# Experts and second attention ordered by batch in a four-block transformer kernel

## Chip, cores and metric

The kernel runs on one core of a Trainium2 chip. The metric is the device time of one execution in microseconds (us), the median of several runs.

## The reference

The input has B = 2 sequences of S = 1024 tokens with D = 128 features. Four blocks follow each other, each of the form x = x + layernorm(block(layernorm(x))):

```
x = x + ln(attn0(ln(x)))     # 16 heads of 64, causal softmax
x = x + ln(moe(ln(x)))       # 8 experts, top 2, capacity 1.25, gelu, F = 256
x = x + ln(attn1(ln(x)))     # 16 heads of 8, rotary q and k, causal; a score of exactly 0 is masked
x = x + ln(ffn(ln(x)))       # ternary weights, squared relu, low-rank term
```

The second attention:

```
q, k = rope(x @ Wq), rope(x @ Wk);  v = x @ Wv          # 16 heads of 8
scores = q @ k.T / sqrt(8) * tril;  scores = where(scores == 0, -inf, scores)
out = softmax(scores) @ v @ wo.T
```

The router ranks a token among all tokens of both sequences (an expert keeps the first CAP of them), so routing needs all of x. Nothing after routing mixes the two batches.

## The kernel before

The kernel is written per engine: TensorE (`pe`), VectorE (`dve`), ScalarE (`act`), GpSimd (`pool`) and the DMA queue of SyncE (`sp`) each have an instruction list in a fixed order, tied by semaphores. Tokens are handled in 16 tiles of 128; a PSUM bank holds 4 tiles (512 tokens, 2 KB per partition), so the two batches are 4 banks (`NB`), and `bank[0..7]` are the eight PSUM banks.

Attention 0 (to 562 us) and its output projection and norms are not touched. After them the router (VectorE) picks experts.

**Experts.** For each of 8 experts `up(e)` makes 8 bank products (2 feature chunks x 4 token banks) in banks 0 to 3 in turn, ScalarE applies gelu into `hT` (double buffered), `down(e)` makes four banks 4 to 7, and VectorE adds each, weighted, into `acc` (`weighted_sums`). TensorE's order is `up(e+1)`, `down(e)`. All 2048 tokens go through one expert before the next. Experts 1 to 6 run in a hardware loop of two per turn on each engine; in it VectorE copies the weights' column and the bias column of the expert (`wcol`, `b1e`). SyncE loads w1 and w2 of the expert after next.

**Between experts and attention 1.** Norm 2 (`norm_stage(2, ...)`): moments and scaling of the experts' sum, GpSimd's power for 1/sqrt and its addition to X, then moments and scaling of X to `xn`. TensorE transposes a bank of it, ScalarE copies it to `xnT`, TensorE makes five projections per bank (q, q with swapped halves, k, k swapped, v), ScalarE copies each from PSUM (`rot`, `V1`). For each of four arrays i (q and k of batch 0, q and k of batch 1, 1024 columns each) VectorE multiplies by the cosine (L996), GpSimd the swapped one by the sine (L533), VectorE adds (L1002). The sum is split in three bf16 parts: ScalarE casts a part (`part`, L667), VectorE subtracts it (`left`, L991), and again; the last part is VectorE's own. The parts are stored to DRAM (`split`), and `stacks(b, g)` loads the part products of a group of 4 heads: 18 loads of 64 KB that fill `QS[:, b]` and `KS[:, b]` (72 partitions, all 9 pairs of parts). So scores of 8 features become one bf16 matmul over 72 rows.

**Attention 1** is 256 items (group of heads, batch, query tile, head). Per step i: TensorE scores(i); VectorE `mask` (L818) makes `Zb`, a large negative number where a score is zero, and `maximum` (L833) adds it and takes the row maximum; ScalarE the exponential (L605) into `probs`; TensorE transposes them (L1133), ScalarE copies them to `PT` (L585), and after every fourth item TensorE multiplies by V. One group of heads takes 64 items: batch 0 with its query tiles rising, then batch 1 with them falling. Thus both batches must be ready before the first group is done. `self.rounds` lists everything that goes through the three PSUM banks `pT`, and `at_step` the step of each.

Order before: group 0 batch 0, group 0 batch 1, group 1 batch 0, and so on. `NMASK = 4` buffers hold `Zb` and `Sm`.

The block after (norm 3, feed-forward, norm 4) is not touched.

Of the kernel before, what the change touches and what calls it, by code (L numbers as in the profile page):

```python
# [7 lines left out]

# [14 lines left out]
P = 128  # L23
B, S, D = 2, 1024, 128
T = B * S
# [21 lines left out]
PROJ1 = (0, 1, 2, 3, 6, 7)  # L47
QUEUED = 4
NMASK = 4
# [32 lines left out]

class Attention:
# [3 lines left out]
    def __init__(self, heads, turns, copies, project):  # L87
# [3 lines left out]
        self.order = [(c, b, qt) for c in range(turns) for b, qt in order]  # L91
        self.items = [(c, b, qt, h) for c, b, qt in self.order for h in range(heads)]
# [12 lines left out]
        for step in range(self.n + 8):  # L105
# [5 lines left out]
            if project:  # L111
                c, at = divmod(step, self.per)
                for c2, b2, start in ((c, 1, 1), (c + 1, 0, self.per // B + 1)):
                    u, odd = divmod(at - start, 2)
                    if 0 <= u < 6 and not odd and c2 < turns:
                        self.project(step, c2, b2, u)
            self.done_by.append(dict(self.copied))
# [4 lines left out]
    def add(self, step, what, args, engines):  # L122
        for e in engines:
            self.copied[e] += 1
        self.at_step[step].append(len(self.rounds))
        self.rounds.append((what, args, {e: self.copied[e] for e in engines}))

# [37 lines left out]
def build(nc, x, w0, wo0, router_w, router_b, w1, b1, w2, b2, wl1, wo1, fast_bT, w_fc, w_proj, uT, v, gate,  # L165
          consts, rotary, out):
    with ExitStack() as ctx:
# [28 lines left out]
        hT = at(0, "hT", [P, 2, FC0, T])  # L196
# [11 lines left out]
        Sm = at(48, "Sm", [P, NMASK, S])  # L208
        cs = at(56, "cs", [P, 2, S])
        QS = at(64, "QS", [P, B, HPG, S], BF16)  # L210
        KS = at(80, "KS", [P, B, HPG, S], BF16)
        rot = at(96, "rot", [P, 8, S])
        PT1 = at(96, "PT1", [P, 2, HPG, S])
        parts = at(136, "parts", [P, 2, PARTS, S], BF16)
# [32 lines left out]
        wcol = sb("wcol", [P, 2, NT])  # L247
# [9 lines left out]
        b1e = sb("b1e", [P, 2, FC0])  # L257
# [52 lines left out]
        rope, rope_sin, part_a, part_v, part_stored = sem("rope"), sem("rope_sin"), sem("part_a"), sem("part_v"), [sem("part_stored0"), sem("part_stored1")]  # L310
        ld_stack = [sem("ld_stack0"), sem("ld_stack1")]

        b1_ready = sem("b1_ready")
# [7 lines left out]
        wcol_ready = sem("wcol_ready")  # L321
# [8 lines left out]
        L = [Attention(HPC, CH0, ["act", "dve"], True), Attention(HPG, G1, ["act"], False)]  # L330
        block = ctx.enter_context(nc.Block())
# [3 lines left out]
        def _(sp):  # L335
# [63 lines left out]
            sp.dma_start(cs[:, :, :], rotary).then_inc(ld_rot, 16)  # L399
            sp.dma_start(wo1s[:, :, :], wo1).then_inc(ld_wo1, 16)  # L400

            with sp.Fori(0, E // 2 - 1) as t:
                for e in range(2):
                    sp.wait_ge(up_done, (t * 2 + e) * UNITS + UNITS)
                    sp.dma_start(w1s[:, e, :], w1[bass.ds(t * 2 + 2 + e, 1), :, :].rearrange("o p f -> p (o f)")).then_inc(ld_w1[e], 16)
                    sp.wait_ge(down_done, (t * 2 + e) * NB + NB)
                    sp.dma_start(w2s[:, e, :, :], w2[bass.ds(t * 2 + 2 + e, 1), :, :].rearrange("o (c p) d -> p (o c) d", p=P)).then_inc(ld_w2[e], 16)
            def stacks(b, g):
# [5 lines left out]
                for i in range(PARTS):  # L414

                    for j in range(PARTS):
                        row = (i * PARTS + j) * DH1
                        sp.dma_start(QS[row:row + DH1, b, :, :], heads(0, slice(i, i + 1)).rearrange("k d h s -> (k d) h s"))\
                            .then_inc(ld_stack[b], 16)
                        sp.dma_start(KS[row:row + DH1, b, :, :], heads(1, slice(j, j + 1)).rearrange("k d h s -> (k d) h s"))\  # L420
                            .then_inc(ld_stack[b], 16)

            for i in range(2):
                sp.wait_ge(part_a, 2 * i + 2)
                sp.wait_ge(part_v, 2 * i + 2)
                sp.dma_start(split[i, :, :, 0:S].rearrange("k p s -> p k s"), parts[:, i, :, :]).then_inc(part_stored[i], 16)
            for b in range(B):
                for i in range(2):  # L430
                    sp.wait_ge(part_stored[i], 16 * (b + 1))
                stacks(b, 0)
            for g in range(G1 - 1):
                for b in range(B):
                    sp.wait_ge(A[1]["s"], g * L[1].per + (b + 1) * L[1].per // B)
                    stacks(b, g + 1)
# [8 lines left out]
        def _(pool):  # L445
# [83 lines left out]
            powers(2)  # L529
            pool.wait_ge(ld_rot, 16)  # L530
            for i in range(4):
                pool.wait_ge(proj1_copied, 5 * (i // 2 * 2 + 1) + i % 2 * 2 + 2)
                pool.tensor_tensor(rot[:, 2 * i + 1, :], rot[:, 2 * i + 1, :], cs[:, 1, :], ALU.mult).then_inc(rope_sin, 1)  # L533
# [5 lines left out]
        def _(act):  # L539
# [23 lines left out]

            def factors_out(a, g):
# [4 lines left out]
            def attention(k):  # L569
                a, plan = A[k], L[k]  # L570
                PT = PT0 if k == 0 else PT1
                def rounds_out(i):
                    for r in plan.at_step[i]:
# [4 lines left out]
                        if what == "P":  # L578
                            projected(a, args, pT[r % TBANKS][:, :])
                            continue  # L580
# [28 lines left out]
                for i in range(plan.n + QUEUED + 1):  # L609
# [5 lines left out]
                    else:  # L615
                        rounds_out(i)
                        exponential(i)

# [20 lines left out]
            def gelus(e, buf):  # L639

                act.wait_ge(b1_ready, e + 1)
                for u in range(UNITS):
                    f, j = u % FC0, u // FC0
                    act.wait_ge(up_done, e * UNITS + u + 1)
                    nc.scalar.activation(hT[:, buf, f, j * BANK:(j + 1) * BANK], bank[u % 4], ACT.Gelu,  # L645
                                         bias=b1e[:, buf, f:f + 1]).then_inc(h_ready, 1)

            gelus(0, 0)
# [687 lines left out]
```

## Time and profile before

| | before |
|---|---|
| median of 3 runs | 1271.85 us (1269.1 to 1274.05) |
| profiled execution, its own time | 1276.66 us |
| its span in the trace | 1274.7 us |
| busy over the span: TensorE / VectorE / ScalarE / GpSimd | 1114.3 / 869.6 / 817.2 / 348.9 us |
| mean granted TensorE clock | 0.955 of full speed |
| experts (first `up` after routing to last sum) | 625.9 to 732.5 us |
| gap from the experts to the first scores of attention 1 | to 801.7 us |
| attention 1, to its output projection | to 1209.6 us |

A busy share says how long an engine had an instruction under way. Its average over the kernel mixes stages with different limits; the rows below are therefore taken by stretch. The granted clock has two levels: 1.00 is 2.4 GHz and 0.50 is 1.2 GHz.

### The profile page before, as it was taken

To read this page: it belongs to the slowest core of one execution; us is meant where nothing else is said; L and a number is where in the kernel's file an instruction comes from. 1 tells how busy PE (TensorE), PEld (TensorE's weight loads), DVE (VectorE), ACT (ScalarE), POOL (GpSimd) and SP (SyncE) were. 2 spreads that over 40 slices of the span, in tenths; PEclk is the share of its full clock that TensorE was granted. 3 is DMA by queue.
4 is the path that set the end of the run, shared out by engine and by line. 5 is a ranking of instruction groups with operands and counts; after the bars stand their busy time and mean duration, and the time that the engine had idled before them with its cause. 6 is when DMAs were issued, how large, how long until landed. Compare 5 with 4: busy or idle time off the path is not lost.

```text
span 1274.7 us, 28360 instructions
## 1 busy us (share of the span) xinstructions
PE 1114.3 (87%) x10202; PEld 850.3 (67%) x10202; DVE 869.6 (68%) x2512; ACT 817.2 (64%) x1915; POOL 348.9 (27%) x345
## 2 busy tenths in 40 slices
PE   2799999999999999998999951688888888888886
PEld 1587888787878787888676730456556556556674
DVE  3565656565656665645433476799899999999863
ACT  2566666666666666631434223789889989989832
POOL 1597464646464545313000051000000000000033
PEclk9899999999999999998899976799899999899998
DMA  3222232323232222211000004311302202100001
GB/s 107 70 60 62 69 73 59 83 57 84 57 76 66 69 72 68 67 35 42 5 17 25 5 1 118 56 24 17 39 12 29 38 4 37 27 14 2 2 1 33
DMA packets 29671, 56.74 MB, mean 45 GB/s; under 512 B 4538, under 2 KB 14674, under 8 KB 29410
## 3 DMA queue, kind: packets, MB, share of 16 engines
q1 hardware_dynamic: 28738, 53.43, 18.8%
q8 instruction: 80, 1.31, 0.4%
q10 hardware_dynamic: 800, 1.57, 0.4%
q14 instruction: 53, 0.43, 0.1%
HBM read 25.49 MB, written 4.33 MB: 23 GB/s over the span
## 4 chain that ended last, share of the span: by engine, by line
PE 55%; DVE 19%; issue 11%; ACT 6%; POOL 5%; DMA 3%; SPq 1%; ACTq 0%; POOLq 0%; DVEq 0%
PE pT L1133 12%; PE pO L1063 11%; PE pS L1100 10%; DVE Zb L818 9%; PE pS L1195 4%; PE pT L1025 4%; PE pT L1207 3%; DVE Sm L833 3%; ACT probs L605 3%; PE pS L1156 2%; PE pT L1029 2%; PE pS L1293 1%; PE pS L1273 1%; ACT PT L585 1%; DMA KS<-split 1%
## 5 line engine op out<-in xcount | busy, mean ns | idle before, releaser
L1133 PE MATMUL pT<-cst,probs 128*128 128x128 f32 x2304 | 368.8, 286 | 55.2 <-ACT probs L605 53.2
L1133 PEld LDWEIGHTS pT<-cst,probs 128*128 128x128 f32 x2304 | 255.5, 142 | 151.9 <-ACT probs L605 104.0
L605 ACT ACTIVATE probs<-probs,nmax 128x128 f32<-128x128 f32 (+7 forms) x256 | 198.8, 776 | 131.7 <-DVE nmax L828 130.7
L585 ACT COPY PT<-pT 128x512 f32<-128x512 f32 (+3 forms) x576 | 263.7, 481 | 16.1 <-PE pT L1133 14.7
L828 DVE CUSTOM_DVE_ANT_0 probs<-pS,causal_wide 128x128 f32<-128x128 f32 (+7 forms) x256 | 192.1, 750 | 92.8 <-PE pS L1100 85.2
L1063 PE MATMUL pO<-PT,V 128*64 128x128 f32 (+1 forms) x4608 | 230.6, 277 | 1.9 <-DVE attnT L787 1.1
L605 ACT ACTIVATE probs<-Sm,nmax 128x128 f32<-128x128 f32 (+7 forms) x256 | 199.2, 778 | 29.3 <-DVE nmax L833 22.3
L818 DVE TENSOR_SCALAR Zb<-pS 128x128 bf16<-128x128 f32 (+7 forms) x256 | 192.8, 753 | 24.4 <-PE pS L1106 24.1
L461 POOL TENSOR_TENSOR rstd<-rstd,power 128x4 f32<-128x4 f32 x32 | 32.8, 1025 | 628.0 <-DVE rstd L725 627.4
L1063 PEld LDWEIGHTS pO<-PT,V 128*64 128x64 f32 (+1 forms) x4608 | 179.9, 113 | 33.8 <-issue 19.6
L833 DVE CUSTOM_DVE_ANT_0 Sm<-pS,Zb 128x128 f32<-128x128 f32 (+7 forms) x256 | 193.3, 755 | 4.5
L862 DVE COPY PT<-pT 128x256 f32<-128x256 f32 (+3 forms) x192 | 99.9, 520 | 115.9 <-PE pT L1133 114.5
L1100 PE MATMUL pS<-Kh,Qs 128*128 128x512 f32 (+2 forms) x384 | 159.0, 423 | 7.2 <-DMA Kl<-Kl 7.2
L1100 PE MATMUL pS<-KS,QS 72*128 72x512 bf16 (+3 forms) x384 | 109.0, 338 | 36.0 <-DMA KS<-split 31.9
L1100 PE MATMUL pS<-Kl,Qs 128*128 128x512 f32 (+2 forms) x384 | 128.8, 344 | 0.0
L1100 PEld LDWEIGHTS pS<-Kh,Qs 128*128 128x128 f32 x384 | 73.3, 191 | 27.8 <-issue 21.7
L1100 PEld LDWEIGHTS pS<-Kl,Qs 128*128 128x128 f32 x384 | 73.5, 191 | 20.3 <-issue 14.6
L645 ACT ACTIVATE hT<-pS,b1e 128x512 f32<-128x512 f32 x64 | 43.9, 687 | 57.5 <-PE pS L1195 57.3
L504 POOL TENSOR_TENSOR Kl<-raw,Kh 64x512 fp32r<-64x512 f32 x60 | 76.5, 1276 | 4.8
L504 POOL TENSOR_TENSOR Ql<-raw,Qs 64x512 fp32r<-64x512 f32 x60 | 76.5, 1275 | 4.8
L524 POOL TENSOR_TENSOR attnT<-attnT,wq_t 128x1024 f32<-128x1024 f32 x16 | 37.9, 2370 | 117.6 <-DMA wq_t<-factors 117.0
L976 DVE SCALAR_TENSOR_TENSOR acc<-pT,wcol,acc 128x128 f32<-128x128 f32 x96 | 27.0, 344 | 61.7 <-PE pT L1207 61.7
(185 smaller groups left out, 1376.2 us busy)
## 6 DMA issues: line engine op xcount, KB each, us to landing
Qs<-Ql SPq DMA_DIRECT2D x32, 256.0 KB, 3.7
Kh<-Kh SPq DMA_DIRECT2D x32, 256.0 KB, 3.4
Kl<-Kl SPq DMA_DIRECT2D x32, 256.0 KB, 4.6
wq_t<-factors SPq DMA_DIRECT2D x32, 256.0 KB, 3.9
QS<-split SPq DMA_DIRECT2D x72, 64.0 KB
KS<-split SPq DMA_DIRECT2D x72, 64.0 KB
w0s<-in_w SPq DMA_DIRECT2D x8, 192.0 KB, 4.1
split<-parts SPq DMA_DIRECT2D x2, 768.0 KB, 3.5
```

The costliest lines, as they stand in the source:

```text
L504: i = pool.tensor_tensor(low[h], source[rows[h], :], high[h].bitcast(F32), ALU.subtract)
L585: nc.scalar.copy(PT[:, g % 2, h, k0 * P:(k0 + nk) * P], pT[r % TBANKS][:, 0:nk * P])\
L605: nc.scalar.activation(probs[:, i % NPROB, 0:n], src[:, 0:n], ACT.Exp, bias=nmax[:, i % 4:i % 4 + 1], scale=-1.0, accum_out=total).then_in ...
L818: nc.vector.tensor_scalar(Zb[:, i % NMASK, 0:n], pS[i % 2][:, 0:n], 0.0, MASKED, ALU.is_equal, ALU.mult).then_inc(a["z"], 1)
L828: nc.vector.tensor_tensor_reduce(probs[:, i % NPROB, 0:n], pS[i % 2][:, shift(k, qt):shift(k, qt) + n], causal_wide[:, S - n:S], -1.0, 3e3 ...
L833: nc.vector.tensor_tensor_reduce(Sm[:, i % NMASK, 0:n], pS[i % 2][:, 0:n], Zb[:, i % NMASK, 0:n], -(DH1 ** -0.5), 3e38, ALU.add, ALU.min, ...
L862: nc.vector.tensor_copy(PT[:, gg % 2, hh, k0 * P:(k0 + nk) * P], pT[r % TBANKS][:, 0:nk * P])\
L1025: return nc.tensor.matmul(p, w0s[:, what, :], xnT[:, b * S + j * BANK:b * S + (j + 1) * BANK], start=True, stop=True)
L1063: m = nc.tensor.matmul(pO[rows, 0:P], v, PT[:, g % 2, h, kt * P:(kt + 1) * P], start=(kt == 0), stop=(kt == qt), skip_group_check=True)
L1100: m = nc.tensor.matmul(pS[i % 2][:, (off + c0) * P:(off + c1) * P], lhs, keys[:, b, h, c0 * P:c1 * P], start=(n == 0), stop=(n == len(rhs) ...
L1133: m = nc.tensor.transpose(pT[r % TBANKS][:, kt * P:(kt + 1) * P], probs[:, item % NPROB, (k0 + kt) * P:(k0 + kt + 1) * P], ident)
L1195: nc.tensor.matmul(bank[u % 4], w1s[:, buf, f * P:(f + 1) * P], xnT[:, j * BANK:(j + 1) * BANK], start=True, stop=True).then_inc(up_done, 1)
```

## The change

The experts run over batch 0 (m = 0 to 7) and then over batch 1 (m = 8 to 15), each step with half the tokens: 4 banks of `up`, 2 of `down`. While batch 1 is in the experts, batch 0 goes through norm 2, transposes, projections, rotation, split and stacked loads. Attention 1 takes all four groups of batch 0 and then all of batch 1; norm, projections, rotation and split of batch 1 are written into the steps of its first 64 items, by tables.

- The hardware loops and the copies `wcol` and `b1e` are gone; weights are loaded 16 times instead of 8 in all (14 after the first two).
- From m = 8 on `up` uses banks 0 and 1 alone, `down` banks 4 and 5 (before m = 8: 0 to 3, and 4 to 7 in pairs). Banks 2 and 3, then 6 and 7 serve transposes and projections.
- ScalarE casts the parts of batch 0 between the gelus of expert steps 13 and 14 (first part) and 14 and 15 (second).
- `QS` and `KS` have two buffers as before, now for this half and the next one of the order. `rot`, `parts` and others have new places in SBUF; `NMASK` is 3 to make room.
- SyncE waits for both stores of batch 0 and then issues stacks(0) and stacks(1) one behind the other. The stores of batch 1 follow stacks(2). Before, ScalarE's queue stored batch 1.

Core of the diff:

```diff
-NMASK = 4
+NMASK = 3
+NORM_STEPS = {1: ("ym", 2), 2: ("ym", 3), 4: ("yn", 2), 5: ("yn", 3), 7: ("xm", 2), 8: ("xm", 3), 10: ("xn", 2), 11: ("xn", 3)}
+ROTATE_STEPS = {38: ("cos", 2), 39: ("cos", 3), 41: ("add", 2), 42: ("add", 3), 44: ("left", 2, 0), 47: ("left", 2, 1),
+                53: ("left", 3, 0), 57: ("left", 3, 1)}
+PART_STEPS = {43: (2, 0), 46: (2, 1), 51: (3, 0), 55: (3, 1)}
+SECOND_BATCH = collections.defaultdict(list)
+for _j in (2, 3):
+    SECOND_BATCH[11 + _j].append(("N", _j))
+    for _what in range(5):
+        SECOND_BATCH[16 + 2 * ((_j - 2) * 5 + _what)].append(("Q", (_j, _what)))
...
+        if heads > 2:
+            self.order = [(c, b, qt) for b in range(B) for c in range(turns) for qt in (tiles if c % 2 == 0 else reversed(tiles))]
...
+            store(0)
+            store(1)
+            sp.wait_ge(part_stored, 32)
+            stacks(0)
+            stacks(1)
+            for half in range(2, G1 * B):
+                sp.wait_ge(A[1]["s"], (half - 1) * (L[1].per // B))
+                if half == G1:
+                    sp.wait_ge(part_stored, 64)
+                stacks(half)
+                if half == 2:
+                    store(2)
+                    store(3)
...
+            for m in range(1, B * E):
+                gelus(m)
+                if m == E + 3:
+                    for j in range(2):
+                        act.wait_ge(tr_done[2], j + 1)
+                        nc.scalar.copy(xnT[:, j * BANK:(j + 1) * BANK], bank[2 + j]).then_inc(xnT_ready[2], 1)
+                if m in (E + 3, E + 4):
+                    j = m - E - 3
+                    for what in range(5):
+                        u = j * 5 + what
+                        act.wait_ge(proj1, u + 1)
+                        projected1(j, what, bank[PROJ1[u % len(PROJ1)]]).then_inc(proj1_copied, 1)
+                if m in (E + 5, E + 6):
+                    part(0, m - E - 5)
+                    part(1, m - E - 5)
...
+            for m in range(E):
+                sums(m, (0, 1))
+            for what in ("ym", "yn", "xm", "xn"):
+                second_norm(what, 0)
+                second_norm(what, 1)
+                if what != "xn":
+                    sums(E + "ym yn xm xn".split().index(what) // 2, ("ym yn xm xn".split().index(what) % 2,))
+            sums(E + 1, (1,))
+            sums(E + 2, (0, 1))
+            sums(E + 3, (0, 1))
+            rotate("cos", 0)
+            rotate("cos", 1)
+            sums(E + 4, (0, 1))
+            rotate("add", 0)
+            rotate("add", 1)
+            left(0, 0)
+            left(1, 0)
+            sums(E + 5, (0, 1))
+            left(0, 1)
+            left(1, 1)
+            sums(E + 6, (0, 1))
+            sums(E + 7, (0, 1))
...
+            for m in range(B * E):
+                if m + 1 < B * E:
+                    up(m + 1)
+                if m == E + 2:
+                    pe.wait_ge(h_ready, E * per_batch)
+                    for j in range(2):
+                        transpose1(j, bank[2 + j]).then_inc(tr_done[2], 1)
+                down(m)
+                if m in (E + 2, E + 3):
+                    j = m - E - 2
+                    pe.wait_ge(xnT_ready[2], 2)
+                    pe.wait_ge(added, NT + E * ST)
+                    for which in range(5):
...
+                        project1(j, which, bank[PROJ1[u % len(PROJ1)]]).then_inc(proj1, 1)
```

`second_norm`, `rotate` and `left` are the pieces of the norm, the rotation and the split as before, one bank or one array at a time. In the inner loop of TensorE, "N" transposes a bank of the normalized batch 1 and "Q" makes one projection, both through `pT`; ScalarE copies them out in its own list.

## Rows read from the trace of the kernel before

**Rows 1.** Busy time by stretch (us, instructions): TensorE, its weight loads, VectorE, ScalarE, GpSimd; clock, DMA.

```profile
732.00:803.00 71.00, 23.26 (x86) 13.25 (x86) 45.56 (x127) 21.27 (x33) 23.48 (x16) 0.68 0.23 62
803.00:1209.00 406.00, 347.69 (x4156) 241.87 (x4154) 387.73 (x955) 370.64 (x961) 0.00 (x0) 0.96 0.16 22
```

**Rows 2.** Chain that ended last, experts: start us, us, engine, output, line, instructions.

```profile
625.90 7.06 PE pS L1195 x16
...
654.12 6.87 PE pS L1195 x16
660.99 5.36 PE pT L1207 x48
...
668.13 6.87 PE pS L1195 x16
```

**Rows 3.** Timeline, a gelu and the last weighted sum (start us, us, idle before).

```profile
626.99 0.69 ACT L645 ACTIVATE hT<-pS,b1e 128x512 f32<-128x512 f32 x1 [4.12 <-PE pS L1195]
...
731.37 1.13 DVE L976 SCALAR_TENSOR_TENSOR acc<-pO,wcol,acc 128x128 f32<-128x128 f32 x4 [0.66 <-PE pO L1207]
```

**Rows 4.** Timeline of VectorE, norm 2.

```profile
732.41 0.86 DVE L718 BATCH_NORM_STATS2 stats<-acc 128x6 f32<-128x128 f32 x4
...
733.80 0.86 DVE L718 BATCH_NORM_STATS2 stats<-acc 128x6 f32<-128x128 f32 x4
...
735.19 1.11 DVE L731 TENSOR_SCALAR yn<-acc,mv,rstd 128x128 f32<-128x128 f32 x4
736.21 0.86 DVE L718 BATCH_NORM_STATS2 stats<-acc 128x6 f32<-128x128 f32 x4
```

**Rows 5.** Timelines of VectorE, ScalarE and GpSimd, rotation and split.

```profile
758.08 0.59 ACT L683 COPY rot<-pS 128x512 f32<-128x512 f32 x1 [0.27 <-PE pS L1260]
758.80 4.85 POOL L533 TENSOR_TENSOR rot<-rot,cs 128x1024 f32<-128x1024 f32 x2 [7.91 <-ACT rot L683]
...
764.66 1.21 DVE L996 TENSOR_TENSOR rot<-rot,cs 128x1024 f32<-128x1024 f32 x1
764.77 1.05 ACT L667 CAST parts<-rot 128x1024 bf16<-128x1024 f32 x1 [2.21 <-DVE rot L1002]
765.85 1.23 DVE L991 TENSOR_TENSOR rot<-rot,parts 128x1024 f32<-128x1024 f32 x1
```

**Rows 6.** Timelines, from the last split pass of batch 0 to the first scores.

```profile
776.21 1.23 DVE L991 TENSOR_TENSOR parts<-rot,parts 128x1024 bf16<-128x1024 f32 x1
...
781.05 0.29 SPq L418 DMA_DIRECT2D QS<-split  x1
...
801.73 0.26 PE L1100 MATMUL pS<-KS,QS 72*128 72x128 bf16 x1 [31.88 <-DMA KS<-split]
```

**Rows 7.** Busy time by stretch around one set of stacked loads in the attention.

```profile
850.00:852.00 2.00, 2.00 (x47) 1.72 (x38) 2.00 (x3) 1.95 (x5) 0.00 (x0) 1.00 0.49 87
...
866.00:868.00 2.00, 1.45 (x12) 0.94 (x10) 2.00 (x6) 1.98 (x5) 0.00 (x0) 1.00 0.36 50
```

**Rows 8.** Busy time by stretch: items 0 to 15, 16 to 31, 32 to 51.

```profile
802.00:820.50 18.50, 14.97 (x120) 8.85 (x119) 15.46 (x57) 15.28 (x48) 0.00 (x0) 0.74 0.54 65
820.50:853.40 32.90, 28.36 (x331) 19.29 (x330) 32.63 (x63) 29.24 (x67) 0.00 (x0) 1.00 0.06 11
853.40:891.90 38.50, 33.48 (x458) 25.05 (x456) 38.16 (x78) 36.73 (x84) 0.00 (x0) 1.00 0.21 25
```

**Rows 9.** Waits in attention 1: total us, times, longest.

```profile
ACT probs L605 <- DVE nmax L833: 22.3, 77, 0.5
```

**Rows 10.** TensorE and ScalarE around routing, and the clock after the experts.

```profile
609.43 9.14 PE L1195 MATMUL pS<-xnT,w1s 128*128 128x512 f32 x16
...
615.18 0.69 ACT L645 ACTIVATE hT<-pS,b1e 128x512 f32<-128x512 f32 x1 [0.17 <-PE pS L1195]
...
618.89 0.23 PE L1217 MATMUL pT<-selb,upperb 128*128 128x128 bf16 x1 [0.32 <-DVE beforeb L936]
...
736.00:737.00 1.00, 0.00 (x0) 0.00 (x0) 1.00 (x6) 0.00 (x0) 1.00 (x2) 0.69 0.00 0
```

More of the change, by code:

```diff
@@ L116, in __init__ @@
                         self.project(step, c2, b2, u)
+            if not project:
+                for r, args in SECOND_BATCH[step]:
+                    self.add(step, r, args, ["act"])
             self.done_by.append(dict(self.copied))
@@ L1005, in _, with sums @@
-            dve.wait_ge(proj1_copied, 20)
+            def sums(m, banks):
+                for j in banks:
+                    dve.wait_ge(down_done, m * 2 + j + 1)
+                    dve.wait_ge(added, NT + ((m - 1) * ST + (j + 1) * TPB if m % E else 0))
+                    for t in range(TPB):
+                        n = m // E * ST + j * TPB + t
+                        nc.vector.scalar_tensor_tensor(acc[:, n, :], bank[down_bank(m, j)][:, t * P:(t + 1) * P],
+                                                       wgt[:, n, m % E:m % E + 1], acc[:, n, :], ALU.mult, ALU.add).then_inc(added, 1)
@@ L1214, in _, with up @@
-            up(0, 0, first=True)
+            def up(m):
+                pe.wait_ge(ld_w1[m % 2], 16 * (m // 2 + 1))
+                for u in range(per_batch):
+                    f, j = u % FC0, m // E * 2 + u // FC0
+                    if m >= 1:
+                        pe.wait_ge(h_ready, m * per_batch + u - 1 if m > E or u >= 2 and m == E else m * per_batch + u - 3)
+                    nc.tensor.matmul(bank[u % 4 if m < E else u % 2], w1s[:, m % 2, f * P:(f + 1) * P],
+                                     xnT[:, j * BANK:(j + 1) * BANK], start=True, stop=True).then_inc(up_done, 1)
@@ new lines, in down @@
+            def down(m):
+                pe.wait_ge(ld_w2[m % 2], 16 * (m // 2 + 1))
+                for j in range(2):
+                    last = m - 2 if m <= E else m - 1
+                    pe.wait_ge(h_ready, m * per_batch + FC0 * (j + 1))
+                    pe.wait_ge(added, NT + (last * ST + (j + 1) * TPB if last >= 0 else 0))
+                    for t in range(TPB):
+                        for f in range(FC0):
+                            n = j * TPB + t
+                            i = nc.tensor.matmul(bank[down_bank(m, j)][:, t * P:(t + 1) * P],
+                                                 hT[:, m % 2, f, n * P:(n + 1) * P], w2s[:, m % 2, f, :],
+                                                 start=(f == 0), stop=(f == FC0 - 1))
+                    i.then_inc(down_done, 1)
```

341 lines of the change are left out of this document (159 added, 182 removed).

## Prediction

> **What bounds the kernel now.** I read the profile from the stages inward. The busy table by stretch [rows 1] has the two stretches that the change touches. Between 732 and 803 us TensorE works 23.3 of 71 us: nothing there keeps any engine full. From 803 to 1209 us, the second attention, VectorE is busy 387.7 of 406 us, ScalarE 370.6, TensorE 347.7: VectorE sets the pace, and what is added to it there costs nearly its own length.
>
> Before 732 us the chain that ended last is TensorE alone [rows 2]: an `up` of 8 banks takes 6.87 us, a `down` of 4 banks 668.13 - 660.99 = 7.14, one expert 14.01 us. Halved for one batch: `up` 3.44, `down` 3.57, expert 7.01; one bank of `down` 1.79. VectorE adds a bank in 1.13 us, and the last one starts at 731.37; a gelu takes 0.69 us and starts right behind its bank [rows 3].
>
> The gap itself is a string of latencies. The norm of a bank [rows 4] is moments 733.80 - 732.41 = 1.39 us and the scaling 736.21 - 735.19 = 1.03, each done twice (for the output and for the next input): 4.84 us a bank. Then come projections, and the rotation with its split in three parts [rows 5]: on VectorE four passes of 1024 elements, 765.85 - 764.66 = 1.19 us each, ScalarE's casts 1.05, GpSimd's product with the sine 4.85 / 2 = 2.43, a projection's copy 0.59. Last come the stores and stacked loads [rows 6]: the second store of batch 0 is released by the pass that ends at 776.21 + 1.23 = 777.44, the loads start at 781.05 (3.6 us later), and TensorE begins at 801.73, after 31.88 idle us that end with a stacked load.
>
> **The change, step by step.** Experts run batch by batch. Up to the boundary nothing but the grain changes: eight half experts, 8 x 7.01 = 56.1 us from 625.90, so at 682.0. The shorter `up(0)` lies under the router on VectorE, thus it gives nothing; the other 15 halves are 105.2 of `up` and `down` in a longer loop than before by half an `up`, 3.4 us. Weights are loaded 14 times instead of 6, 128 KB each, on an otherwise idle queue, with at least 7 us from issue to use; free.
>
> Then I lay out batch 1, counting from t = 0 at 682.0, with these durations. TensorE: `up(9)` and `down(8)` to 7.0, `up(10)`, `down(9)` to 14.0, `up(11)` to 17.5. VectorE meanwhile: last sum of expert 7 to 1.2, two moments to 3.9, sum (5.3 to 6.4), two scalings to 8.5, sum to 9.5, moments to 12.3, sum to 13.4, scalings to 15.5, sum to 16.6. The transposes at 17.5 find their inputs ready, and `down(10)` its bank. So the norm of batch 0, 9.7 us of VectorE, costs TensorE no wait. Transposes 1.2, `down(10)` to 22.3, five projections at 0.86 (one bank of `up`, 6.87 / 8) to 26.6; `up(12)`, `down(11)` to 33.6, five projections to 37.9; `up(13)`, `down(12)` to 44.9.
>
> Here comes the one wait I find. VectorE's sum ends at 46.1 and only then its two additions of the rotation, at 47.3 and 48.5. ScalarE stands in order before the gelus of expert 14 with two casts that wait for these: they end at 49.5. With two banks left to `up`, TensorE's third bank waits until 50.3 where it would have started at 46.6: 3.6 us. `up(14)` ends at 52.0, `down(13)` at 55.6, its sum at 56.7, then the last two passes of the split at 57.9 and 59.1. Two banks instead of four also cost some 0.25 us per expert, since a bank's gelu ends 0.14 + 0.69 us after the bank and the other bank takes 0.86; with hand-overs I add 2.1 us for the six experts up to here. The second store is released at 682.0 + 61.2 = 743.2, the stacked loads start 3.6 us later, 746.8.
>
> How long do 18 stacked loads take? With two stores beside them, 801.73 - 781.05 = 20.7 us; in the attention, alone, transfers go from the slice at 850 into the one at 866 [rows 7], about 17.5. I take 19.2: attention starts at 766.0 in place of 801.7, **35.7 us sooner**. The experts end on TensorE at 682.0 + 68 = 750, so it is the split and its loads that are late, by 16 us, not the experts.
>
> Batch 1's own work now goes into VectorE's attention: norms of two banks, 9.7 us, and 8 passes, 8 x 1.19 = 9.6 us: 19.3. Of it some 2 us fall on the first small tiles, where VectorE is idle 3.0 of 18.5 us in the first row of [rows 8]: 17.3. ScalarE gets 2 + 10 copies and 4 casts, 12 x 0.59 + 4 x 1.05 = 11.3 us. In steps 16 to 31 (second row of [rows 8]) it is busy 29.2 of 32.9 us, and nine copies, nearer 0.5 each where they overlap, put it at 33.7. TensorE is busy 28.4 there, and nine of the ten projections at 0.86 put it at 36.1, in front of both; as its busy time counts the modelled tail of each group, I take a bit less: +3.0. In the falling half behind it (its third row) VectorE carries the 9.6, ScalarE has 36.7 + 4.7 and TensorE 33.5 + 0.9 of 38.5 + 9.6: no cost. Two casts stand one step ahead of the pass that needs them, and there VectorE waits about 0.6 us each: +1.2. Three masks for four: in the waits of this stretch ScalarE waits 77 times for VectorE's maximum [rows 9], so it isn't three items behind; nothing. The loads of later halves have 50 us each. Sum in the attention: 17.3 + 3.0 + 1.2 = **+21.5**.
>
> Bounds: the loads 17.5 to 20.7; hand-overs and the 3.6 us wait between 0 and 8; the inserted work from 15.6 (19.3 less the 3.7 us that VectorE is idle in the three rows, and nothing else) to twice the 17.3.
>
> Sum: -35.7 + 21.5 = -14.2. The profiled execution took 1276.66 us (span 1274.7 and 2.0 around it), 4.8 over the median of 1271.85. So 1262.5 for a like execution, and 1257.7 as median, **1258**.
>
> **The rivals.**
> 1. The inserted work is hidden better: VectorE's idle 3.7 us take their part, ScalarE and TensorE keep up, the one-step waits vanish, and the loads take 17.5. For it: VectorE does idle while TensorE makes scores. Against: most of that idle time is in the smallest tiles. I take 8 us for the three: 1250.
> 2. TensorE's clock falls. `up(0)` is half as long: the gelu of its fourth bank started at 615.18, and the matmul that ranks tokens came at 618.89: some 3.9 idle us where the old `up(0)` filled them. The granted clock fell from 2.4 to 1.2 GHz some 5 us after the matmuls that ended at 731.3 (0.69 in the slice 736 to 737) [rows 10]. If it falls in this gap, the b2 products and the next `up` run slower. The old `up(0)` began in the low state and took 9.14 against 6.87 us at the full one; I take 3 us. 1261. A gap of 3.6 us before the third bank could do the same once more.
>    The Trainium skill (TensorE: Matmul & The Clock Gate, What's actually happening) calls the low rate the default, which only activity lifts; by that rule the clock falls in this gap, and the median is this rival's 1261. Whether a gap so short suffices, no row here shows.
> 3. Three engines are nearly full in the attention (388, 371, 348 of 406 us), and each inserted piece breaks their rhythm: a chunk of 1.4 us on VectorE makes ScalarE late, then TensorE's transposes, then the next scores. If that doubles the cost of 17 us, 1258 + 17 = 1275, no change.
> 4. The other side. The stacked loads of the second half now follow those of the first without a pause, 36 where 18 went. While 18 are under way the DMA engines are about half busy (0.49 in the slice at 850), so two sets could share them. If the two sets run interleaved, attention starts after both: 41.4 us for 19.2, and 1258 + 22 = 1280, slower. From 14.2 us above my 19.2 on, the gain is gone. Against it: one queue, issued in order, and before the change two stores pushed in between cost at most 3 us.
>
> **How the numbers follow.** My forecast 0.60, rival 1: 0.10, rival 2: 0.12, rival 3: 0.10, rival 4: 0.08. The range reaches to rival 1 and a bit beyond (1248) and most of the way to rival 3, whose milder half is inside: 1248 to 1273. Outside are rival 4, the other half of 3 and a lower tail. The line of 0.5% (6.4 us, about what a measurement of this kernel can tell from no change) lies at 1265.5. Forecast, 1 and 2 are below it, less 0.05 for their upper tails: faster 0.77. Most of rival 3 and the tails: same 0.13. Rival 4 and a bad end of 3: slower 0.10.
>
> **What would show it.** The boundary between batches at 682, TensorE full with one wait of 3 to 4 us in `up(14)`, released by a gelu behind casts; experts ending at 750; the first stacked load issued near 747 and the first scores near 766, TensorE idle 16 us in between. The attention from there to the output projection 429 us instead of 408, all the excess in its first two halves (about 50 each before), the other six unchanged. Wrong would be: scores only after some 785 (rival 4), more than 435 us of attention (rival 3), the clock at half after 620 (rival 2).

## The result and the profile after

The changed kernel takes 1258.2 us (median of 4 runs, 1254.7 to 1264.2) against 1273.0 for the kernel before in the same runs: the ratio is 0.989, with a 95% interval of 0.984 to 0.994. The forecast was 1258, with a range of 1248 to 1273. The profiled execution of the changed kernel is its shortest (1254.74 us, span 1252.9) and that of before one of the longer ones, so the two traces stand 21.8 us apart where the medians stand 14.7 apart. The comparison by stage must therefore say which stretches the change touched at all.

Busy time by stretch, after (us, instructions: TensorE, weight loads, VectorE, ScalarE, GpSimd; granted clock, DMA share, GB/s). The stretches are experts of batch 0, experts of batch 1, the wait for the stacked loads, the first two halves of the attention, and its other six:

```profile
626.00:684.65 58.65, 58.65 (x327) 41.94 (x326) 18.05 (x62) 21.98 (x32) 0.00 (x0) 0.97 0.11 32
684.65:753.30 68.65, 65.22 (x353) 44.22 (x351) 38.99 (x124) 31.10 (x45) 12.43 (x8) 0.98 0.16 51
753.30:769.30 16.00, 0.06 (x2) 0.07 (x2) 1.29 (x5) 0.00 (x0) 0.00 (x0) 0.58 0.55 72
769.30:890.35 121.05, 101.42 (x1073) 68.77 (x1074) 116.30 (x296) 100.81 (x251) 11.29 (x8) 0.87 0.17 33
890.35:1191.60 301.25, 255.49 (x3130) 178.53 (x3128) 291.61 (x724) 276.68 (x726) 0.00 (x0) 0.99 0.15 21
```

The 71 us of [rows 1] in which no engine was full have become 16. VectorE is busier in the second row than in the first (39.0 for 18.1 us), with the norm, rotation and split of batch 0, and TensorE is still full but for 3.4 us. In the attention VectorE is the busiest engine in both rows, 116.3 of 121.1 us in the first.

The timeline of TensorE after, at the end of the experts (start us, us, idle time before and its releaser):

```profile
735.30 3.65 PE L1299 MATMUL pS<-xnT,w1s 128*128 128x512 f32 x4 [3.43 <-ACT hT L729]
...
742.39 3.79 PE L1299 MATMUL pS<-xnT,w1s 128*128 128x512 f32 x8
746.01 7.31 PE L1312 MATMUL pT<-w2s,hT 128*128 128x128 f32 x64
769.26 0.27 PE L1198 MATMUL pS<-KS,QS 72*128 72x128 bf16 x1 [15.94 <-DMA KS<-split]
```

and those of VectorE, ScalarE and SyncE beside it:

```profile
731.23 2.35 DVE L866 TENSOR_TENSOR rot<-rot 128x1024 f32<-128x1024 f32 x2
732.48 2.18 ACT L639 CAST parts<-rot 128x1024 bf16<-128x1024 f32 x2 [5.18 <-DVE rot L866]
734.57 1.26 ACT L729 ACTIVATE hT<-pS,b1s 128x512 f32<-128x512 f32 x2
...
743.64 2.35 DVE L871 TENSOR_TENSOR parts<-rot,parts 128x1024 bf16<-128x1024 f32 x2
746.92 1.28 ACT L688 ACT_TABLE_LOAD   x1
750.50 0.30 SPq L464 DMA_DIRECT2D QS<-split  x1
```

These answer to [rows 5, 6]. The third bank of `up(14)` waits 3.43 us for a gelu; that gelu (734.57) stands behind two casts, and these behind the two additions of the rotation. The last split pass ends at 743.64 + 2.35 = 745.99, the loads start 4.5 us later and take 769.26 - 750.50 = 18.8 us, and TensorE waits 15.94 us for them. It starts 32.5 us sooner than before. One row holds something that was not forecast: ScalarE loads the table of the exponential at 746.92, far ahead of the first scores; before, this load stood between the first scores and the first exponential. The row before:

```profile
802.87 1.28 ACT L605 ACT_TABLE_LOAD   x1 [14.77 <-DVE nmax L833]
```

The attention has eight halves of 32 items. Taken from the first mask of each half to that of the next, they last 59.9, 60.8, 50.3, 50.1, 49.1, 50.1, 49.1 and 52.6 us (to the output projection) after; before, 51.2, 50.1, 51.8, 50.1, 49.1, 50.1, 52.1 and 53.0. So the inserted work costs 8.7 + 10.7 = 19.4 us between these two traces, and 4.9 us of the difference lie in halves that do the same as before. The two touched halves, the first before and after, then the second before and after:

```profile
802.00:853.40 51.40, 43.34 (x448) 28.14 (x447) 48.09 (x117) 44.52 (x114) 0.00 (x0) 0.91 0.23 30
769.60:829.55 59.95, 51.26 (x474) 32.58 (x472) 58.10 (x167) 47.38 (x123) 8.92 (x7) 0.83 0.15 22
853.40:903.50 50.10, 43.13 (x588) 32.06 (x585) 48.56 (x123) 48.08 (x123) 0.00 (x0) 1.00 0.16 20
829.55:890.35 60.80, 49.86 (x601) 35.91 (x599) 58.20 (x130) 53.43 (x129) 2.37 (x1) 0.92 0.20 43
```

VectorE's busy time grows by 10.0 and 9.6 us. The 10.7 of the second half is the figure of one execution: in the ten other profiled executions that hold all of batch 1's work on VectorE this half took 60.1 to 62.7 us (the first always 59.9), with VectorE busy 58.1 to 58.3 us in each and the clock at 1.2 GHz for a different share of the time. Against 50.1 before, the second half thus costs 10.0 to 12.5 us.

### The profile page after: what moved, and what is told of

Its sections match the earlier page's. It is cut to its first block, busy times and chain, and to the rows that moved or that the text cites. A ratio compares the mean times of both kernels' runs of the same rounds, so it can differ in the third digit from the quotient of the medians.

```text
span 1252.9 us, 28180 instructions
## 1 busy us (share of the span) xinstructions
PE 1112.5 (89%) x10202; PEld 844.8 (67%) x10202; DVE 862.9 (69%) x2486; ACT 814.4 (65%) x1915; POOL 349.4 (28%) x345
## 4 chain that ended last, share of the span: by engine, by line
PE 56%; DVE 18%; issue 11%; ACT 7%; POOL 5%; DMA 3%; SPq 1%; ACTq 0%; POOLq 0%; DVEq 0%
PE pT L1237 12%; PE pO L1160 12%; PE pS L1198 10%; DVE Zb L914 9%; PE pS L1299 4%; PE pT L1108 4%; PE pT L1312 3%; ACT probs L688 3%; DVE Sm L929 3%; PE pS L1260 2%; PE pT L1112 2%; ACT PT L668 1%; PE pS L1379 1%; PE pS L1359 1%; DMA KS<-split 1%
## 5 line engine op out<-in xcount | busy, mean ns | idle before, releaser
L688 ACT ACTIVATE probs<-Sm,nmax 128x128 f32<-128x128 f32 (+7 forms) x256 | 199.4, 779 | 61.2 <-DVE nmax L929 55.4
L914 DVE TENSOR_SCALAR Zb<-pS 128x128 bf16<-128x128 f32 (+7 forms) x256 | 192.7, 753 | 21.5 <-PE pS L1204 21.2
L1198 PEld LDWEIGHTS pS<-Kl,Qs 128*128 128x128 f32 x384 | 73.5, 191 | 20.3 <-issue 14.6
L729 ACT ACTIVATE hT<-pS,b1s 128x512 f32<-128x512 f32 x64 | 43.7, 687 | 57.2 <-PE pS L1299 57.2
L1064 DVE SCALAR_TENSOR_TENSOR acc<-pT,router,acc 128x128 f32<-128x128 f32 x112 | 31.5, 344 | 66.1 <-PE pT L1312 66.1
```

What stands on the lines that cost most here:

```text
L688: nc.scalar.activation(probs[:, i % NPROB, 0:n], src[:, 0:n], ACT.Exp, bias=nmax[:, i % 4:i % 4 + 1], scale=-1.0, accum_out=total).then_in ...
L914: nc.vector.tensor_scalar(Zb[:, i % NMASK, 0:n], pS[i % 2][:, 0:n], 0.0, MASKED, ALU.is_equal, ALU.mult).then_inc(a["z"], 1)
L1198: m = nc.tensor.matmul(pS[i % 2][:, (off + c0) * P:(off + c1) * P], lhs, keys[:, b if k == 0 else half % 2, h, c0 * P:c1 * P], start=(n == 0),
```

## Experiments

### Undoing the clock's fall

The granted clock after, in slices of 2 us from the end of `up(0)`:

```profile
614.00:616.00 2.00, 0.21 (x1) 0.00 (x0) 1.73 (x11) 0.76 (x2) 0.00 (x0) 1.00 0.26 66
616.00:618.00 2.00, 0.06 (x1) 0.07 (x2) 1.69 (x11) 0.00 (x0) 0.00 (x0) 1.00 0.00 0
618.00:620.00 2.00, 0.95 (x7) 0.51 (x8) 1.11 (x5) 0.00 (x0) 0.00 (x0) 0.86 0.00 0
620.00:622.00 2.00, 2.00 (x11) 1.23 (x10) 0.00 (x0) 1.23 (x3) 0.00 (x0) 0.50 0.03 8
```

TensorE is idle from 614.2 to 617.94, and its clock falls from 2.4 to 1.2 GHz in the slice at 618. That is rival 2. `e1_fill` fills the gap:

```diff
             up(0)
+            pe.wait_ge(ld_w1[1], 16)
+            for u in range(4):
+                nc.tensor.matmul(bank[7], w1s[:, 1, 0:P], xnT[:, 0:BANK], start=True, stop=True)
             pe.wait_ge(r_, 8 + NT)
```

> The changed kernel with four extra products of 512 columns on TensorE right behind up(0), so that it isn't idle while VectorE routes (their result is not used). Clock theory (rival 2 of the prediction): the granted clock stays at full from 614 us on, up(1) takes 3.4 us instead of 5.1, and the first up of batch 1 starts 3 to 4 us sooner against routing's end (684.65 - 617.94 = 66.7 us between the ranking product and the end of the eighth down in the changed kernel; 63 to 64 expected). Rival theory, that the longer stretch has another cause (weight loads, waits for sums): unchanged at 66.7. Total: 3 us less than the changed kernel, some 1255.

Measured: 1258.1 us, not to be told from the changed kernel. The first projection comes 87.4 us after the ranking product (704.94 - 617.50), in the changed kernel 89.0 (706.95 - 617.94). So filling gives 1.6 us there, half of what was expected. The changed kernel's clock falls twice, in the slices at 618 and 626 (0.86 and 0.56, with 1.00 at 624 between them). Filling removes the first fall and not the second, which comes after the transposes and the products over 8 rows, with TensorE busy all the time by its records (in `e1_fill` the slice at 626 is at 0.50).

What each fall costs can be read from the same products at either clock, first in the changed kernel, then in `e1_fill`:

```profile
619.27 2.61 PE L1325 MATMUL pT<-cst,router 128*8 128x128 f32 x12 [1.05 <-DVE router L1048]
621.68 1.06 PE L1325 MATMUL pO<-cst,router 128*8 128x128 f32 x4
626.68 5.17 PE L1299 MATMUL pS<-xnT,w1s 128*128 128x512 f32 x8
...
618.84 1.48 PE L1328 MATMUL pT<-cst,router 128*8 128x128 f32 x12 [1.05 <-DVE router L1048]
620.15 0.60 PE L1328 MATMUL pO<-cst,router 128*8 128x128 f32 x4
624.44 5.40 PE L1299 MATMUL pS<-xnT,w1s 128*128 128x512 f32 x8
633.25 3.60 PE L1299 MATMUL pS<-xnT,w1s 128*128 128x512 f32 x8
```

The first fall costs 3.67 - 2.08 = 1.6 us, the second 5.17 - 3.60 = 1.6 (1.8 in `e1_fill`): together 3.2 us in the changed kernel. In the four other profiled executions with the gap where the clock was back by 624, the distance was 89.0 to 89.3 us. In two (`e3_late` and `e6_pe8`, the same up to here) the clock stayed low to about 634, and it was 93.2 and 92.3 us. The slice at 630 in `e6_pe8`:

```profile
630.00:632.00 2.00, 2.00 (x3) 0.70 (x3) 0.39 (x1) 0.36 (x1) 0.00 (x0) 0.50 0.00 0
```

Against `e1_fill` the gap thus costs 1.6 to 5.7 us, differing from execution to execution; the second fall, which filling leaves, comes on top.

`e8_up1` fills it with work that is needed anyway:

```diff
             up(0)
+            up(1)
             pe.wait_ge(r_, 8 + NT)
...
-                if m + 1 < B * E:
+                if 0 < m and m + 1 < B * E:
                     up(m + 1)
...
             gelus(0)
+            gelus(1)
```

> The changed kernel with up(1) ahead of the routing products instead of behind them, so that eight banks of up lie under VectorE's routing as before the change. Clock theory: TensorE's idle time of 3.7 us there is filled with work that was needed anyway, so 3.4 us less behind routing, and the clock stays up as in the kernel before (1.6 us less than the changed kernel and up to 5 in its slower executions). First projection 84 us behind the ranking product (89.0 in the changed kernel, 87.4 with filling products); median 5 us less, 1253. Rival (ScalarE's gelus delay its copies for routing): 2 us or less.

Measured: 1255.5 us, ratio to before 0.985 (0.981 to 0.989). The first projection comes at 84.9 us (702.79 - 617.87), 4.1 less than in the changed kernel, near the 84 expected. Of these, 3.6 us are `up(1)` itself, no longer behind routing; the second fall of the clock came here too (0.56 in the slice at 626). As the profiled execution had 21.1 us of loads instead of 18.8, its first scores come only 1.9 us sooner.

### Which chain sets the start of the attention

`e2_early` moves VectorE's pieces, nothing else:

```diff
             rotate("cos", 1)
-            sums(E + 4, (0, 1))
             rotate("add", 0)
             rotate("add", 1)
+            sums(E + 4, (0, 1))
             left(0, 0)
             left(1, 0)
-            sums(E + 5, (0, 1))
             left(0, 1)
             left(1, 1)
+            sums(E + 5, (0, 1))
```

> The changed kernel with VectorE's two rotation additions ahead of the sums of step 12 and the last split passes ahead of the sums of step 13. Theory (the chain norm, projections, rotation, split, loads of batch 0 sets the start of the second attention, the experts don't): the 3.4 us wait of TensorE in up(14) is gone, the last split pass ends 8 us sooner (738 for 746), the first scores come 8 us sooner (761 for 769), the median falls by 8 us. Rival (the experts' end or the loads behind set the start): the wait goes but the first scores move by less than 4 us.

Measured: 1255.7 us, ratio to before 0.989 (0.985 to 0.993). TensorE's wait in `up(14)` is gone. VectorE's timeline in it:

```profile
735.74 2.36 DVE L871 TENSOR_TENSOR parts<-rot,parts 128x1024 bf16<-128x1024 f32 x2 [1.88 <-ACT parts L639]
738.02 2.15 DVE L1064 SCALAR_TENSOR_TENSOR acc<-pT,router,acc 128x128 f32<-128x128 f32 x8
```

The last split pass ends at 738.1, 7.9 us sooner, as expected; but the first scores come at 764.9, only 4.4 sooner. The rest went in two places behind it. From the split to the first load 5.7 us pass for 4.5, because SyncE issues the stores in order behind the last w2 load, which waits for `down(13)`; and the loads took 21.1 us for 18.8. So the chain of the split does set the start, but not all of what it gains arrives. My expectation of 8 us was too high by these two.

### What sets the time of 18 stacked loads

`e3_late` holds the second set back until the first scores:

```diff
             stacks(0)
+            sp.wait_ge(A[1]["s"], 1)
             stacks(1)
```

> The changed kernel, but the 18 loads of the second half are issued only after the first scores. Rival 4 of the prediction (the two sets share the DMA engines): the first 18 loads land clearly sooner than the 18.8 us of the changed kernel, and the first scores come sooner. Theory (one queue, in order): 18 to 19 us as before, no change of the median.

Measured: 1258.7 us; the loads take 775.54 - 754.81 = 20.7 us. Rival 4 is out: without the second set behind them they are not shorter (18.8 in the changed kernel, 21.0 to 21.1 in the five other executions of this order with one queue and the second set behind).

`e4_twoq` issues the nine loads of keys from ScalarE's queue, which is idle there:

```diff
+                        if half == 0:
+                            continue
                         sp.dma_start(KS[row:row + DH1, half % 2, :, :], heads(1, slice(j, j + 1)).rearrange("k d h s -> (k d) h s"))\
                             .then_inc(ld_stack[half % 2], 16)
...
+            act.wait_ge(part_stored, 32)
+            for i in range(PARTS):
+                for j in range(PARTS):
+                    row = (i * PARTS + j) * DH1
+                    act.dma_start(KS[row:row + DH1, 0, :, :],
...
+                        .then_inc(ld_stack[0], 16)
             attention(1)
```

> The changed kernel, with the nine loads of keys of the first half issued by ScalarE's queue instead of SyncE's. If the 18.8 us are set by one queue working through 18 loads one behind the other, they fall to some 10 to 12 us and the median by 7 us. If they are set by the DMA engines that hold these rows (half of them were busy), they stay at 18 us and nothing changes. I give the first 0.5.

Measured: 1258.8 us. In its timeline both queues issue from 751.21, and the scores come at 769.4:

```profile
751.21 3.42 SPq L464 DMA_DIRECT2D QS<-split  x10
...
769.40 0.26 PE L1207 MATMUL pS<-KS,QS 72*128 72x128 bf16 x1 [15.37 <-DMA KS<-split]
```

18.2 us, and 18.5 in `e7_best` below, which loads in the same way. That is next to nothing against the 18.8 of the changed kernel, but that execution is an exception: the eight others with one queue, two of them in the old order, took 20.3 to 21.1. So a second queue is worth between nothing and some 3 us, not the 7 of the expectation, and what it is worth stays open; the medians (1258.8 for 1258.2) don't tell.

Then `e9_cols` asks whether it is bytes or rows:

```diff
-            stacks(0)
+            stacks(0, slice(0, BANK), ld_first)
+            stacks(0, slice(BANK, S))
             stacks(1)
...
-                    if k == 1 and i % (plan.per // B) == 0:
+                    if k == 1 and i == 0:
+                        pe.wait_ge(ld_first, 16 * 2 * PARTS * PARTS)
+                    if k == 1 and (i == TPB * HPG or i > 0 and i % (plan.per // B) == 0):
```

> The changed kernel, with the first half's stacked loads in two sets: columns 0 to 511 of all 18 first (scores of item 0 wait for these alone), then columns 512 to 1023 (item 16 waits for them). Rows of 1 KB instead of 2 KB. If the loads are set by bytes, the first scores come after 9 to 10 us instead of 18.8 (or 21), and the median falls by 9 us. If they are set by the number of rows moved, both sets take 18 us each, the first scores come as before, and the second set is late or just in time for item 16 (some 26 us later): no change or slower. I give bytes 0.4.

Measured: 1250.5 us, ratio to before 0.983 (0.980 to 0.986). From the first load (749.55) to the first scores (760.63) 11.1 us pass, for half the bytes in the same number of rows. So the bytes count and not the rows alone, though not in proportion: half the bytes take 0.59 of 18.8 us, and a quarter (`e11_sets` below) 7.6 us, of which the issues alone take 6.2. While whole sets are under way the engines are half busy and move some 72 GB/s (third row of the first table). And the rising half needs only the first columns for its first 16 items. The first two halves keep their length (59.9 and 61.6 us), so item 16 does not wait.

### What the inserted work costs

`e5_dve8` shrinks VectorE's pieces for batch 1 and keeps their waits: in moments and scalings one tile with 8 columns, in the rotation and the first split pass 8 columns. So batch 1 is left mostly uncomputed.

```diff
-                nc.vector.tensor_tensor(to, rotated(i, 0), part_of(i)[:, j, :], ALU.subtract).then_inc(part_v, 1)
+                c = slice(0, S if i < 2 or j == 1 else 8)
+                nc.vector.tensor_tensor(to[:, c], rotated(i, 0)[:, c], part_of(i)[:, j, c], ALU.subtract).then_inc(part_v, 1)
```

> The changed kernel, leaving out nearly all of VectorE's work for batch 1 inside the attention: moments and scalings of one tile with 8 columns instead of four with 128, cosine, addition and first split pass on 8 columns instead of 1024, with all waits and the last split passes kept (so batch 1 is computed from other numbers). The inserted VectorE work falls from 19.3 to about 5 us. Theory (VectorE sets the pace, inserted work costs its own length): the first two halves of the attention, 120.7 us in the changed kernel, fall by 13 to 15 us, the first half by about 7, the second by 7. Rival 3 (rhythm broken by waits and by the other engines): they fall by less than 8 us.

Measured: 1247.6 us. The first two halves take 53.7 + 55.7 = 109.4 us, 11.3 less than after. VectorE's busy time in them:

```profile
772.50:826.30 53.80, 50.20 (x475) 33.06 (x473) 51.28 (x131) 47.49 (x123) 8.94 (x7) 0.86 0.19 25
826.30:882.00 55.70, 45.65 (x601) 33.73 (x600) 52.07 (x130) 52.91 (x129) 2.37 (x1) 1.00 0.23 48
```

It fell by 116.3 - 103.4 = 12.9 us, and the time by 11.3. That is short of the 13 to 15 I expected, but over the 8 of rival 3. The first half is the cleaner test, as its length was 59.9 us in all eleven executions with the full work, at whatever clock: 6.2 us less for 6.8 us of busy time, so VectorE's inserted work costs nearly its length. In the second half (5.1 us less) the clock is at 1.00, where the changed kernel had 0.92, so some of that can be the clock's. There ScalarE also comes up to VectorE once VectorE's part is gone (52.9 to 52.1).

`e6_pe8` shrinks TensorE's pieces for batch 1 instead (one transpose of four, projections of 8 columns), so batch 1 is transposed and projected only in part:

```diff
-                for t in range(TPB):
+                for t in range(TPB if j < 2 else 1):
...
+                if j >= 2:
+                    return nc.tensor.matmul(p[:, 0:8], wl1s[:, which, :], xnT[:, j * BANK:j * BANK + 8], start=True, stop=True)
```

> The changed kernel, leaving out most of TensorE's work for batch 1 inside the attention: one transpose instead of four per bank and projections of 8 columns instead of 512 (ScalarE's copies stay full). Theory of the prediction (in steps 16 to 31 TensorE and ScalarE come in front of VectorE, +3.0 us): the first half, 59.9 us, falls by 2 to 3 us. Rival (VectorE stays in front, the projections are hidden): by less than 0.7 us.

Measured: 1264.1 us, 5.9 more than the changed kernel, with less work. The two profiled executions are 11.5 us apart, and of these 3.3 lie behind routing, where the clock stayed low, 2.3 in the loads and 1.9 in the second half; whether the other executions were alike, nothing shows. The first half takes 59.85 us, as with the full projections. So the projections are hidden, and the rival holds: VectorE stays in front. TensorE's busy time there fell only from 51.3 to 49.4 us, though nine projections at 0.86 us were all but taken out.

`b1_nmask3` is the kernel before with `NMASK = 3`.

> The kernel before with three mask buffers instead of four. Theory: no wait of VectorE for a buffer, so the attention takes 407.8 us and the median is that of before within noise. Rival: VectorE waits for the exponential, at least 3 us more.

Measured: 1272.4 us, ratio 1.000 (0.998 to 1.002). The third buffer less costs nothing; its attention takes 404.7 us (407.8 before; 2.7 of the difference lie in one rising half, for the clock's sake, last section), its first two halves 51.2 and 50.1 as before.

### Together

`e7_best` joins `e1_fill`, `e2_early` and `e4_twoq`.

> Three edits together on the changed kernel: products behind up(0) to keep the clock, rotation and split ordered earlier, keys of the first half loaded by ScalarE's queue. If all three theories hold: 3 + 8 + 7 = 18 us less, but then the end of the experts (about 745) sets the start of the attention, so 15 us less: 1243. If the loads don't gain by a second queue: 11 us less, 1247.

Measured: 1250.0 us, ratio 0.983 (0.979 to 0.987): 3 us over the forecast for the case that the second queue gives nothing. It is 8.3 below the median of the changed kernel, where the medians of its parts alone had given 0.1, 2.5 and -0.6; with four to six runs each, 5.6 to 10.6 us apart, such medians can't be added up. In the profiled execution the first scores come 10.9 us sooner, 2.1 of them before routing. `e10_all` joins `e8_up1`, `e2_early` and `e9_cols`.

> The changed kernel with up(1) ahead of routing, rotation and split ordered earlier, and the first half's loads in two column sets. Sum of the single effects as far as they hold: 5 + 5 + 9 = 19 us less, cut by the end of the experts, which then comes near the first scores: 1243. If the column sets give nothing: 10 us less, 1248.

Measured: 1239.3 us, ratio 0.974 (0.971 to 0.976). First scores at 748.7, 20.5 us sooner than after (1.3 of them before routing), with TensorE idle for 6.0 us in front of them. `e11_sets` adds two steps:

```diff
+                if m == B * E - 1:
+                    store(0)
+                    store(1)
                 sp.wait_ge(down_done, (m - 1) * (S // BANK))
...
-            stacks(0, slice(0, BANK), ld_first)
+            stacks(0, slice(0, 2 * P), ld_first[0])
+            stacks(0, slice(2 * P, BANK), ld_first[1])
```

> The version with all three edits (up(1) ahead of routing, rotation and split earlier, loads by column sets), with two more steps: the first set is split again (columns 0 to 255 for items 0 to 7, 256 to 511 for items 8 to 15), and the two stores of batch 0 are issued ahead of the last w2 load in SyncE's order, as in that version 5.7 us passed from the last split pass to the first stacked load where 4.5 had. If landing goes on by bytes, the first set lands 6.2 to 7 us after its first issue (the issues alone take 6.2) where 10.5 were measured, and the first scores come 3.5 to 4 us sooner, with 1.2 more from the stores; by then the experts have only just ended, so their end takes over as the bound. Median 1235. If short rows of 512 bytes cost as much each as rows of 1 KB, no gain from the split: 1238.

Measured: 1235.4 us, ratio 0.972 (0.968 to 0.976). The first set lands 7.6 us after its first issue, and the stores stand ahead of the weights:

```profile
730.82 1.51 SPq L450 DMA_DIRECT2D split<-parts  x2
732.38 0.98 SPq L460 DMA_DIRECT2D w2s<-in_w  x1
736.70 0.30 SPq L475 DMA_DIRECT2D QS<-split  x1
```

The experts end at 742.2 and the first scores come at 744.3: the end of the experts now is all but the bound. This version beats the kernel before by 2.8% and the changed one by some 1.8%; its runs (1229.3 to 1240.2) overlap those of `e10_all` (1236.5 to 1240.1), so the last two steps are seen in the trace and not in the medians.

## Why the prediction was right, point by point

- **Grain and boundary.** Forecast: batch 0 out of the experts at 682.0. Measured 684.65, though routing ended 1.0 us earlier in this execution: 3.6 us late. That is rival 2: the clock did fall in the gap behind the shorter `up(0)`. Its mechanism was right and its chance of 0.12 too low: the fall came in all seven profiled executions with the gap and in none of the five where it was filled. Its 3 us measured 1.6 for the fall in the gap, and 3.2 with a second fall at 626. That one has another cause, as it comes with the gap filled and once in the old order (`b1_nmask3`, below). By the rule of the Trainium skill (TensorE: Matmul & The Clock Gate, What's actually happening) the clock falls when activity stops; the trace agrees for the fall in the gap, with 1.00 in the slice at 616 and 0.50 at 620. The second fall, at 626, came with TensorE busy by its records.
- **Batch 1's experts.** The layout held nearly to the microsecond. Counted from the boundary, transposes at 17.9 (forecast 17.5), the wait in `up(14)` 3.43 us (3.6), the last split pass at 61.3 (61.2; the 2.1 us of hand-overs in it stood for the clock, which fell once more behind this wait, to 0.50 in the slice at 736: the last two banks of `up(14)` took 3.65 us, the first two 1.88).
- **Stores and loads.** 4.5 us for 3.6 from pass to first load: the two stores now run at the same time, with the DMA engines full from 746 to 750; 18.8 for 19.2 of loads; 15.94 us of idle TensorE for 16. The loads were luck: every other execution with one queue took 20.3 us or more, over my 19.2. The 17.5 I had read from [rows 7] was short, as that set was issued from 849.3 and its last packet ended 19.2 us later. The start of the attention came 32.5 us sooner where 35.7 were forecast: the 2.7 us of the boundary and the store.
- **Inserted work.** Forecast 21.5 us: 17.3 for VectorE, 3.0 for TensorE in steps 16 to 31, 1.2 for two one-step waits. Measured 19.4. In the second half 10.7 for 10.8: 9.6 us more of VectorE's busy time, and about 1.1 more of its idle time; in the other executions the idle time differs, and it would have been 10.0 to 12.5. In the first half 8.7 for 10.7. **The term of 3.0 us is the step that failed**: `e6_pe8` shows that the projections cost nothing. I had added 0.86 us for each to TensorE's busy time of [rows 8], which counts the modelled tails of short products and so isn't a sum that must fit into the stretch; measured, TensorE is busy 101.4 of 121.1 us. The 7.7 us (17.3 - 9.6) for VectorE's norms in this half were too few: its busy time grew by 10.0, and its idle time fell by only 1.4 (3.3 us before, 1.9 after), where I had hidden 2. Nearly all of that 1.4 can be the exponential's table load, 1.28 us, which left the path and which no step of mine had; no run separates the two. So the measured 8.7 us are made of other parts than my 10.7.
- **The sum.** Touched stretches: -32.5 + 19.4 = -13.1, of which 1.0 lies before routing, where -14.2 was forecast; the medians differ by 14.7. Of the 21.8 us between the two traces, 4.9 more lie in the six other halves and 3.8 behind the attention, neither of which the change touched. For the same reason the attention took 422.3 us where I had forecast 429: 2.1 us less inserted work and 4.9 us less in the six halves that I had called unchanged. That 1258 was hit so closely is in part that a late start (3.2 us) and a cheaper attention (2.1) offset each other.
- **Rivals.** Rival 1 (hidden better) didn't come. Rival 3 is refuted by the 19.4 us themselves, where it would have been some 34, and by `e5_dve8`; rival 4 by the first scores at 769.3 and by `e3_late`.

## What to carry to other kernels

Two phases that are each bound by latency can lie beside a phase that fills another engine, but the pieces cost their own length again wherever they are put on the engine that is full; so put them beside the phase where their engine is idle (here the experts: 20 us of VectorE's work for batch 0 cost TensorE one wait of 3.4 us), and write the layout down with measured durations first. Then look at the order at the end of that chain: casts ahead of gelus, a store behind an unrelated weight load, a load whose first columns would do for the first items. With the gap at routing these held back another 23 us (first scores at 744.3 for 769.3, 1.9 us of it before routing).

When a prefix is shortened since it "lies under" another engine's work, ask what else could stand there: half of `up(0)` less under the router cost a low clock, and `up(1)` in its place gave 4 us, most of it its own length.

## What the runs showed of the hardware

- The clock fell although TensorE was busy by its records: in `e1_fill` TensorE has no idle time from 618.84 us on, and the clock is 0.88 in the slice at 624 and 0.50 in the one at 626, after small transposes and products over 8 rows. The clock fell in this place in ten of the twelve profiled executions of the changed order; in the other two it was low already. In the old order, with more dense products right ahead, it fell in one of two: the kernel before stayed at 1.00 through the same work, but `b1_nmask3`, which is the same up to here, has

```profile
624.00:626.00 2.00, 2.00 (x11) 1.42 (x10) 1.39 (x3) 0.00 (x0) 0.00 (x0) 0.67 0.00 0
```

- The same 18 loads took 20.3 to 21.1 us in eight executions with one queue, in both orders, with and without a second set behind them, and 18.8 in a ninth, the changed kernel's; nothing in the kernels goes with that one. With two queues they took 18.2 and 18.5.
- A rising half of the attention lasts 49.1 to 52.1 us, in kernels with the same work there. Two stretches at the start of the same half, `e10_all` (51.8 us) and after (49.1):

```profile
969.70:979.70 10.00, 8.45 (x55) 4.71 (x54) 8.59 (x40) 8.30 (x34) 0.00 (x0) 0.68 0.55 77
```

```profile
990.70:1000.70 10.00, 7.78 (x77) 4.52 (x76) 9.56 (x43) 8.94 (x37) 0.00 (x0) 1.00 0.56 71
```

  With TensorE's clock at 0.68 of full in the smallest tiles VectorE is busy 8.6 of 10 us, with it at 1.00 9.6. The 42 rising halves without inserted work in the fourteen traces fall in line: 49.0 to 49.1 us where the clock was at 2.4 GHz throughout, 49.7 to 50.3 with some 3 us at 1.2 GHz, 51.0 with some 7, 51.8 to 52.1 with some 10. This accounts for most of the 4.9 us between the two traces in halves that the change left alone (before has some 10 us at 1.2 GHz in two of them), and it is likely much of the spread of some 10 us between executions, of which only one of each kernel has a trace.
